# Two four-row operations in place of four one-row operations with two scalars: the normalised rows that GpSimd writes for the second context attention

## The reference, cut to what matters

```python
def _layernorm(x, axis=-1, eps=1e-05):
    m = jnp.mean(x, axis=axis, keepdims=True)
    v = jnp.var(x, axis=axis, keepdims=True)
    return (x - m) / jnp.sqrt(v + eps)
...
def _L3_xattn_ref(Q, K, V, WQ, WK, WV):
    q = jnp.einsum('bsd,ed->bse', Q, WQ)
    k = jnp.einsum('bsd,ed->bse', K, WK)
    v = jnp.einsum('bsd,ed->bse', V, WV)
    scores = jnp.einsum('bqd,bkd->bqk', q, k)
    causal = jnp.tril(jnp.ones((S, S), dtype=bool))
    scores = jnp.where(causal, scores, 0.0) / math.sqrt(D)
    probs = jax.nn.softmax(scores, axis=-1)
    return jnp.einsum('bqk,bkd->bqd', probs, v)

def _L3_ffn_ref(x, w_gate, w_up, w_down):
    def act_qdq(x):
        scale = jnp.maximum(jnp.max(jnp.abs(x)) / qmax, 1e-12)
        return jnp.clip(jnp.round(x / scale), -qmax - 1.0, qmax) * scale
    x = act_qdq(x)
...
    x = x + jnp.tanh(g_xattn[3]) * _L3_xattn_ref(_layernorm(x, axis=-1), ctx_1024, ctx_1024, ...)
    x = x + jnp.tanh(g_ffn[3]) * _L3_ffn_ref(_layernorm(x, axis=-1), ...)
```

## Time and profile before

| what | value |
|---|---|
| median of 3 runs | 2110.47 us (2106.33 to 2115.61) |
| profiled execution | 2107.25 us |
| its span | 2105.4 us |
| busy: PE, DVE, ACT, POOL | 1896.9, 1637.6, 1292.3, 371.8 us |
| the rows of L1370 | 64 operations of 128x128, between 1682.5 and 1768.9 us of the span |

### The profile page before, as it was taken

The page is one execution under the profiler, slowest core; times in us unless marked ns, Lnnn a source line. Parts: engine busy times, 40 slices in busy tenths (PEclk is TensorE's granted clock), DMA queues, the critical chain, the costliest instruction groups (busy, mean ns, idle before and its releaser), DMA issues. The chain is left out here.

```text
span 2105.4 us, 47401 instructions
## 1 busy us (share of the span) xinstructions
PE 1896.9 (90%) x17713; PEld 1449.0 (69%) x17713; DVE 1637.6 (78%) x4628; ACT 1292.3 (61%) x3167; POOL 371.8 (18%) x679
## 2 busy tenths in 40 slices
PE   7999999999969989999989897999999976899608
PEld 5787787877759988888867574677677765344208
DVE  5787887887859969999957796777777569787894
ACT  4777777777862318888856465455455267109744
POOL 1111111111111114433311142000000096000000
PEclk9999999999988999999989899999999999899859
DMA  5222221111116631111100022322232111002452
GB/s 151 59 67 55 52 59 47 44 45 44 46 53 242 242 132 33 34 34 33 30 1 1 11 60 69 109 83 83 85 120 85 52 41 31 0 0 120 182 177 81
DMA packets 123395, 152.32 MB, mean 72 GB/s; under 512 B 45817, under 2 KB 98594, under 8 KB 121122
## 3 DMA queue, kind: packets, MB, share of 16 engines
q1 hardware_dynamic: 119986, 147.71, 22.6%
q10 hardware_dynamic: 3184, 1.58, 0.3%
HBM read 110.19 MB, written 22.28 MB: 63 GB/s over the span
## 5 line engine op out<-in xcount | busy, mean ns | idle before, releaser
L1783 ACT ACTIVATE arena<-banks,b1c 128x512 f32<-128x512 f32 x192 | 131.5, 687 | 142.4 <-PE banks L1608 140.8
L1712 DVE TENSOR_TENSOR arena<-arena 128x512 f32<-128x512 f32 (+1 forms) x256 | 170.3, 686 | 57.5 <-ACT arena L1783 53.6
L623 ACT ACTIVATE arena<-banks,arena 128x128 f32<-128x128 f32 x512 | 180.1, 372 | 1.2 <-DVE arena L570 1.2
L499 PE MATMUL banks<-arena,wk 128*128 128x128 f32 x1024 | 134.8, 286 | 1.9 <-DVE arena L594 1.9
L1618 PEld LDWEIGHTS banks<-w2a,arena 128*128 128x128 f32 x1024 | 122.0, 192 | 20.1 <-issue 20.1
L499 PEld LDWEIGHTS banks<-arena,wk 128*128 128x128 f32 x1024 | 122.4, 196 | 13.3 <-issue 11.0
L538 PE MATMUL banks<-wv,arena 128*128 128x512 f32 x256 | 131.0, 594 | 0.0
L806 PE MATMUL banks<-we,arena 128*128 128x128 f32 x1024 | 127.5, 283 | 0.6 <-DVE arena L876 0.2
L1618 PE MATMUL banks<-w2a,arena 128*128 128x128 f32 x1024 | 124.7, 275 | 0.0
L806 PEld LDWEIGHTS banks<-we,arena 128*128 128x128 f32 x1024 | 121.3, 196 | 3.6 <-DVE arena L876 3.0
L1608 PE MATMUL banks<-arena,w1s 128*128 128x512 f32 x256 | 123.1, 615 | 0.0
(11 more groups left out here) (261 smaller groups left out, 5052.2 us busy)
## 6 DMA issues: line engine op xcount, KB each, us to landing
arena<-coef_scratch SPq DMA_DIRECT2D x32, 2048.0 KB, 8.3
arena<-arena SPq DMA_DIRECT2D x256, 64.0 KB, 2.0
gated_scratch<-arena SPq DMA_DIRECT2D x16, 768.0 KB, 3.2
arena<-gated_scratch SPq DMA_DIRECT2D x16, 768.0 KB, 4.3
arena<-z1T_scratch SPq DMA_DIRECT2D x128, 64.0 KB, 2.3
arena<-in_ctx_turned SPq DMA_DIRECT2D x32, 256.0 KB, 2.8
arena<-in_ctx SPq DMA_DIRECT2D x64, 64.0 KB, 2.1
z1T_scratch<-arena SPq DMA_DIRECT2D x64, 64.0 KB, 1.6
```

What stands on the lines that cost most here:

```text
L499: mm = pe.matmul(ps[:, n, c * P:(c + 1) * P], k.wk0[:, c * P:(c + 1) * P], Z[t.idx % 3][:, :, n], start=True, stop=True)
L623: act.activation(prob[:, o, c * P:(c + 1) * P], ps[:, SCORES + o, c * P:(c + 1) * P], ACT.Exp, bias=low[:, o, c:c + 1], accum_out=total[:, ...
L1712: dve.tensor_tensor(by_tile, by_tile, wide_coef[g.par][rows, e], ALU.mult).then_inc(s["scaled"].sem, 1)
L1783: act.activation(hT[g.par][:, c, :], ps[:, HID + c % NHID, :], ACT.Gelu, bias=k.b1c[:, c:c + 1])\
```

## The change

For each group the four `tensor_scalar` operations on 128x128 with two scalars for a partition (subtract the mean, multiply by `rstd`) become two `tensor_tensor` operations on 128x512: the first subtracts the mean, given as a 128x4 tensor that is broadcast along the innermost 128 columns, and the second multiplies the result in place by `rstd`, broadcast in the same way. The second waits for the first by a new semaphore, `centred`. The signal `xhat_ready` rises by four once, where it rose by one four times; its readers waited for the fourth already.

```diff
@@ -1329,6 +1329,8 @@
         names["biased" if biased else "masked"] = 1
+        if masked:
+            names["centred"] = 1
         s = k.sigs(G, names)
@@ -1366,10 +1368,12 @@
                     if g.has(2):
                         pool.wait_ge(*f["xT_psum"](g.back(2)))
-                    for j in range(GROUP):
-                        pool.tensor_scalar(xh[g.par][:, j * D:(j + 1) * D], k.x[:, sub(g, j).idx, :],
-                                           mv[g.par][:, j, 0:1], k.rstd[:, j, 0:1], ALU.subtract, ALU.mult)\
-                            .then_inc(f["xhat_ready"].sem, 1)
+                    rows, whole = by_tile(xh[g.par]), [P, GROUP, D]
+                    pool.tensor_tensor(rows, k.x[:, g.idx * GROUP:(g.idx + 1) * GROUP, :],
+                                       mv[g.par][:, :, 0:1].broadcast_to(whole), ALU.subtract).then_inc(s["centred"].sem, 1)
+                    pool.wait_ge(*s["centred"](g))
+                    pool.tensor_tensor(rows, rows, k.rstd[:, :, 0:1].broadcast_to(whole), ALU.mult)\
+                        .then_inc(f["xhat_ready"].sem, GROUP)
```

## The result

| what | before | changed |
|---|---|---|
| median of 7 runs | 2109.99 us (2106.33 to 2116.26) | 2096.95 us (2094.38 to 2100.82) |
| ratio, 95% interval | | 0.9939 (0.9926 to 0.9953) |
| profiled execution, span | 2107.25, 2105.4 us | 2096.95, 2095.1 us |

The changed kernel is 13.0 us or 0.6% faster. The forecast was a gain of 8.0 us, to 2102.5 us.

What follows compares the result with a forecast made beforehand. GpSimd was taken to bound the fourth attention, VectorE 6% behind. Terms gave 3.3 + 7.6 - 0.9 = 10.0 us at the middle price, 7.5 dear, some 7 cheap; 8.0 was taken: 2110.5 - 8.0 = 2102.5 us, range 2096 to 2112.

Steps and rivals of the forecast that it cites:

- What bounds: Fourth attention: GpSimd sets the pace at 6.06 us a group with the next stage's statistics; VectorE needs 5.67, TensorE is behind both.
- The price: GpSimd, each group: the two new operations and their gap cost 2.44 us, 0.69 less than the four old ones' 3.13.
- cheap bound: Both new GpSimd operations at 1.04 us, pair 2.21 us, 0.92 less a group; lead-in gain capped near 3.9 us by TensorE's order.
- the two nearest rows: GpSimd operations used for pricing: L998, multiplication by a mask broadcast innermost, 1.04 us; L1378, addition not broadcast innermost, 1.27 us.
- The rival of a slow subtraction: Subtraction off GpSimd's quick path: 2.6 us, pair 3.8, 0.66 more a group, 10.6 us slower, 2121 us; chance 0.07.
- (a): Lead-in, before VectorE's first update of `x` (L1450): five groups' rows come earlier, gain 3.3 us (bounds 2.3 and near 3.9).
- (b): VectorE's waits in L1983 for GpSimd's power L1919 vanish, since GpSimd's period falls below VectorE's step: gain 7.6 us.
- (c): Shared SBUF port: GpSimd's long two-tensor operations hold up VectorE's L1467, 0.50 us a step when they meet; loss about 0.9 us.
- the middle price: GpSimd pair with one operation at 1.27 us and one at 1.04: 2.44 us together; total gain 10.0 us.
- the first rival: Attention steps with GpSimd in slack: the port takes all the gain, steps of 6.95 us over six to nine steps, 2110 us; chance 0.18.
- the cheap price: Both GpSimd operations at 1.04 us; port losses from the start eat the six short VectorE waits; total gain some 7 us.
- the third rival: All the gain comes through: VectorE's operations slip past the port, 12 us gained, 2098 us; chance 0.15 for over 10.5.

Runs made afterwards that it cites:

- padded kernel: Changed kernel plus one 0.79 us 128x128 subtract-and-multiply on GpSimd per group, into unused columns, ahead of the pair: 2109.25 us, ratio 1.0002 to the kernel before.
- the second trace of the changed kernel: The changed kernel executed and profiled once more, no edit: 2106.10 us, with 108.09 us from the stage's first GpSimd memset to the maximum L1866.

## Why the prediction was right, and where it was off

*What bounds.* Right. GpSimd set the pace in 5% of the span while the page shows it 18% busy. The padded kernel shows it: with the pair kept and GpSimd's length restored, the stretch is that of the kernel before (115.93 against 115.91 and 115.64).

*The price.* I took 1.27 + 0.13 + 1.04 = 2.44 us; measured were 1.04 + 0.14 + 1.04 = 2.22, my cheap bound of 2.21 but for 0.01. With it GpSimd's period while the attention is alone fell to 3.73 us (1687.01 to 1690.74), just below the 3.8 to 4.2 that I had named as the sign. The choice between the two nearest rows was wrong, and so was the reason that I gave for it (broadcast or operation). The rival of a slow subtraction is out. What the Trainium skill ("GPSIMD Engine Reference", section 3.1) gives for two-input operations, about 1.2 us by the prediction's estimate, lies between the 1.27 of the repeated row and the 1.04 of the other forms; no single figure for two-input operations holds here.

*(a) The lead-in.* Taken 3.3 us, measured 4.9 and 3.9 (27.12 to 22.26, 26.86 to 22.97); the cheap bound was 3.9. It is a term that was mis-sized: 0.6 us by the price, and the cap that I put on it for TensorE's order was too low. Of the seven traces whose first groups have the pair at 2.22 us, six have a lead-in of 22.23 to 22.26 us and 1.12 or 1.13 us for the query matmuls shown above; only the second trace of the changed kernel has 22.97 and 2.08. The kernel before has 1.70 and 2.08 us at that place, with lead-ins of 27.12 and 26.86:

```profile
1692.40 1.70 PE L1404 MATMUL banks<-arena,A 128*128 128x512 f32 x2
```

So a later clock cost the kernel before nothing, and went with 0.7 us in the changed one: there TensorE has a part in the pace of the lead-in, which the prediction had named as a sign of being wrong. Whether the change itself makes the clock rise earlier is not shown: none of the four traces with the old length in the first groups has the early rise, and six of the seven with the new length have it, but no run holds the rest fixed.

*(b) VectorE's waits.* Taken 7.6 us, and it came: 7.6 to 0.2 in the windows of the earlier trace rows, 9.6 to 2.0 over the whole trace. A step without a wait is 5.56 us and not 5.67, since operations of VectorE that follow each other without a wait overlap by about 0.1 us: some 1 us more over ten steps, an estimate.

*(c) The port.* Taken 0.9 us at the middle price, measured 3.7. The mechanism was right: under the first rival I had computed 5.67 + 0.50 + 0.78 = 6.95 us a step, L1467 held up and then the copy, and two steps of the first trace last 6.99 us each (1743.59 to 1750.58 to 1757.57). That the numbers agree so well is partly luck: the step without a loss is 5.56 and not 5.67, and the two losses are 0.58 and 0.84 us and not 0.50 and 0.78. GpSimd's two long operations beside them are these:

```profile
1749.33 1.04 POOL L1372 TENSOR_TENSOR arena<-x_tiles,arena 128x512 f32<-128x512 f32 x1
1750.52 1.04 POOL L1375 TENSOR_TENSOR arena<-arena,rstd 128x512 f32<-128x512 f32 x1
```

L1471, begun at 1749.65, ends at 1750.65, so its usual 0.42 us, if they ran in one piece at the end, ran from about 1750.23; the copy ends at 1751.59, so its 0.17 us ran from about 1751.42. Both instants are 0.90 us behind the start of one of the two operations; I had taken 0.78, from L998. Other operations of VectorE beside the pair keep their length: the statistics (L1997 at 1727.63, L698 at 1728.82) take 0.86 and 0.84 us beside the pair of 1727.92 to 1730.14, as in the kernel before, and the update L1454 at 1713.87, one of whose two tensors is in PSUM, takes 1.13 us for its four beside an L1375 at 1713.74, as elsewhere. So it is not that every access of GpSimd slows VectorE. What I had wrong is how often: at the cheap price I expected it from the first joint step, and it takes GpSimd six steps to win enough on VectorE (0.42 us a step, 5.56 less 5.14, once both have reached these periods). The stretched copies and L1471 cost 0.84 + 0.58 + 0.84 + 0.58 + 0.84 = 3.7 us in the first trace, and 1.4 more in the second. Of the 3.8 us that VectorE is busy longer, 2.6 us lie in the joint part (76.93 to 79.56), which fits these 3.7 less the 1 us of overlap of (b), and 1.3 in the lead-in (12.87 to 14.15), where L1471 took 0.98, 0.59 and 1.29 us beside the new pair. The first rival named the right mechanism and too large a reach: three or four steps, not six to nine. The page of the Trainium skill on the port ("SBUF — State Buffer", two separate sides) says that the pair is held for the whole instruction; here L1471 and the copy got through about 0.90 us into operations of 1.04, by the working above.

*The sum.* By the stretch: 4.9 + 7.6 + 1.0 - 3.7 = 9.8 us, the 9.75 measured. My sum at the middle price, 10.0, comes as near by luck: 1.6 us too little in (a) and 1.0 in (b) stand against 2.8 too little in the debit (c). The price that came true was the cheap one, and there the recorded "some 7" does not follow from its own terms: 3.9, the three long waits and the last (1.35 + 1.20 + 1.20 + 1.50 = 5.25), less 1, make 8.2. What it had wrong is that the port would eat the six short waits (2.3 us) from the first step on. The medians differ by 13.0 us, with an interval from 9.9 to 15.6 us (0.74% to 0.47% of 2110). The stretch explains 7.6 to 9.8 of it, just short of the interval; the rest was sought in the parts ahead and behind, which scatter more than that from trace to trace for equal code, and no trace ties it to the change. Whether it is chance stays open.

*The class.* By the bound of 0.5% the kernel is just faster (0.61%, though the interval reaches down to 0.47%), where 0.69 stood on no change that can be told and 0.24 on this; the third rival, all of it coming through at the cheap price for 12 us, was nearest in time, and not for its reason, since VectorE's operations did not slip past.

## What to carry to other kernels

An engine that the page shows at 18% can be the one that sets the pace of a stage; ask for the period of every engine in that stage, and an operation taken from the longest is worth its length until the next engine's period is reached. When GpSimd gets slack beside VectorE, its long operations settle at a fixed place in VectorE's step, and if an operation with two SBUF inputs or a copy stands there, each step can lose more than was won (1.42 us against waits of 0.39 here). Another order of VectorE's step, or a slightly slower GpSimd, can then be better: one trace of each showed a shorter stretch. Where a change moves a few us of 2100, measure the stretch between two marks in the trace and not only the time.

## What the runs showed of the hardware that was not expected

- On GpSimd a `tensor_scalar` with two scalars for a partition costs 0.79 us for 128 columns (L1370), and a `tensor_tensor` 1.04 us for 512: a subtraction with a dense second input, and a subtraction, an addition and a multiplication with one that is broadcast along the innermost dimension. With a 128-column row repeated four times it costs 1.27, as an addition (L1378) and as a subtraction.
- A 128x4 copy on VectorE, 0.17 us by itself, took 1.01 us beside a GpSimd `tensor_tensor` of 1.04: it was held by its neighbour's length, not by its own size.
